# A three-layer graph convolution on one core: four buffers for left-over rows, another order of the work, and the last bias from ScalarE

## What is computed

```python
h = jnp.maximum(_layernorm(x), 0.0)                      # input of conv 1
a = gelu(layer_norm(gcn_conv(h, W1, b1), gamma1, beta1))  # conv 1
c = layer_norm(gcn_conv(a, W2, b2), gamma2, beta2)        # conv 2
x = x + gelu(c + h)
h = jnp.maximum(_layernorm(x), 0.0)
out = x + gcn_conv(h, W3, b3)                             # conv 3
# gcn_conv: segment_sum(dinv[s] * dinv[d] * (x @ W)[s], d) + b, with a self loop for every node
```

## Time and profile before

| | |
|---|---|
| median of the runs | 3902.14 us |
| profiled execution, its own time | 3909.11 us |
| its span (first to last instruction) | 3907.3 us |
| mean granted clock of TensorE | 0.931 |
| busy share of the span: PE, PEld, DVE, ACT, POOL | 79%, 65%, 71%, 46%, 63% |
| instructions | 58757 |
| preamble, about | 0 to 435 us |
| conv 1, about | 435 to 1389 us |
| conv 2, about | 1389 to 2908 us |
| conv 3, about | 2908 to 3907 us |

### The profile page before, as it was taken

How to read it: one execution, slowest core, us unless ns; L and a number is a source line. 1 busy time by engine, 2 the same in 40 slices (tenths; PEclk the granted TensorE clock), 3 DMA queues, 4 the chain that set the end, 5 groups by cost and what they waited for, 6 DMA issues and landing times. The chain is left out here.

```text
span 3907.3 us, 58757 instructions
## 1 busy us (share of the span) xinstructions
PE 3089.9 (79%) x15721; PEld 2521.0 (65%) x15721; DVE 2763.0 (71%) x6384; ACT 1780.0 (46%) x2611; POOL 2449.4 (63%) x1853
## 2 busy tenths in 40 slices
PE   8133599999999957777777777777759999999999
PEld 2122487777777746666666666666647777777777
DVE  9899688778888857666666666666646656566665
ACT  0365466666666635555555555555541122111111
POOL 0122466666666647666666666666648887888877
PEclk9999999999999989888888888888869999999999
DMA  2599777777777747777677677777748888888886
GB/s 108 225 412 416 254 206 197 195 204 198 196 202 196 186 143 217 212 213 202 206 215 209 198 213 213 203 210 210 210 148 246 247 253 255 251 257 252 258 248 202
DMA packets 321118, 867.69 MB, mean 222 GB/s; under 512 B 78801, under 2 KB 79987, under 8 KB 321064
## 3 DMA queue, kind: packets, MB, share of 16 engines
q1 hardware_dynamic: 190120, 682.00, 47.8%
q0 software_dynamic: 130944, 185.08, 26.8%
HBM read 653.10 MB, written 307.81 MB: 246 GB/s over the span
## 5 line engine op out<-in xcount | busy, mean ns | idle before, releaser
L835 POOL DMA_INDIRECT gathered<-H,idx x1062 | 1567.7, 1476 | 430.6 <-issue 253.8
L894 ACT ACTIVATE ahi<-agg 128x1024 fp32r<-128x1024 f32 x354 | 360.7, 1019 | 1136.3 <-PE agg L1184 1099.3
L1204 PE MATMUL out<-Wlo,ahi 128*128 128x512 f32 x2832 | 835.7, 421 | 0.0
L1204 PE MATMUL out<-Whi,ahi 128*128 128x512 f32 x2832 | 834.5, 420 | 0.0
L1204 PE MATMUL out<-Whi,alo 128*128 128x512 f32 x2832 | 792.5, 403 | 26.7 <-DVE alo L1013 26.3
L1184 PE MATMUL agg<-sv,vhi 128*128 128x256 f32 x1416 | 418.1, 323 | 456.2 <-DVE sv L1007 456.0
L1005 DVE TENSOR_TENSOR vlo<-gathered,vhi 128x512 fp32r<-128x512 f32 x354 | 352.3, 995 | 504.5 <-ACT vhi L888 479.4
L1204 PEld LDWEIGHTS out<-Wlo,ahi 128*128 128x128 f32 x2832 | 585.2, 207 | 137.2
L1204 PEld LDWEIGHTS out<-Whi,alo 128*128 128x128 f32 x2832 | 558.5, 199 | 173.2 <-DVE alo L1013 50.6
L1021 DVE BATCH_NORM_STATS2 small<-out 128x6 f32<-128x512 f32 x472 | 317.2, 693 | 435.0 <-PE out L1210 428.9
L1184 PEld LDWEIGHTS agg<-sv,vhi 128*128 128x128 f32 x1416 | 295.3, 209 | 498.3 <-DVE vlo L1005 481.0
(11 more groups left out here) (169 smaller groups left out, 3528.9 us busy)
## 6 DMA issues: line engine op xcount, KB each, us to landing
gathered<-H SPq DMA_DIRECT2D x351, 512.0 KB
H<-ho SPq DMA_DIRECT2D x250, 512.0 KB, 9.5
x<-in_x_dram SPq DMA_DIRECT2D x165, 512.0 KB, 8.7
X<-x SPq DMA_DIRECT2D x117, 512.0 KB
x<-X SPq DMA_DIRECT2D x117, 512.0 KB
out_dram<-conv SPq DMA_DIRECT2D x117, 512.0 KB
H<-x SPq DMA_DIRECT2D x48, 512.0 KB, 9.6
gathered<-H,idx POOLq DMA_INDIRECT x1062
```

What stands on the lines that cost most here:

```text
L835: pool.indirect_dma_start(rows[c], None, H[q][0:N, :], bass.IndirectOffsetOnAxis(ap=own[:, c:c + 1], axis=0), bounds_check=N - 1, oob_is_e ...
L894: nc.scalar.activation(Ahi[p.slot(2)][:, :], Agg[p.slot(2)][:, :], ACT.Copy)\
L1204: m = nc.tensor.matmul(o, a[u][:, c:c + P], w[q][:, f, :], start=(n == 0 and not first), stop=(not second and n == 3 * KD - 1), skip_group ...
```

## The change

- `V` has four buffers in place of two; `gather` is split into `gather_over` (the left-over rows of pair p+4, which wait for `Vlo` of pair p) and, behind it, `gather_first` (the two adding transfers of pair p+3). `v_in` has four semaphores. The row numbers (`indices`) are made five pairs ahead instead of four, and later in DVE's turn.
- The selection matrix is one `tensor_scalar` in place of a `scalar_tensor_tensor` with a tensor of ones.
- Conv 2 on DVE: `over_low(p+2)` is now the first thing of the turn, then `low(p+1)`, `stats(p)`, `indices(p+5)`, and the rest; `normal` is split by halves with `x2_scale` and `x2_shift` between. ACT makes `over_high(p+3)` behind `high(p+2)`. POOL's `residual(p)` waits until DVE has made the selection of pair p+2.
- Conv 3: ACT seeds `Out` with the bias (`seed`), DVE's `result` adds the input rows `Xt` directly, and POOL has no sums left.
- In the preamble the one-hot tiles and `placeb` lie in the new buffers of V, and there are four one-hot tiles instead of three.

```diff
-        gathered = sb("gathered", [P, 10, D])
+        gathered = sb("gathered", [P, 12, D])
-        V = [gathered[:, 8 + u, :] for u in range(2)]
+        V = [gathered[:, 8 + u, :] for u in range(4)]
...
+                    def gather_over(known, p, k):
+                        if has(known, k - 4):
+                            pool.wait_ge(vlo_done.sem, vlo_done.upto(p.after(-4)))
+                        pool.wait_ge(idx_made.sem, idx_made.upto(p))
+                        pool.sem_inc(gather_go, 1)
+                        gather(p, 2, V[p.slot(4)][:, :], v_in, ALU.bypass)
+                    def gather_first(p):
+                        pool.wait_ge(idx_made.sem, idx_made.upto(p))
+                        pool.wait_ge(self_in.of(p), self_in.upto(p))
+                        pool.sem_inc(gather_go, 1)
+                        for j in range(2):
+                            gather(p, j, SelfP[p.slot(4)][:, j, :], g_in, ALU.add)
...
                     def residual(known, p):
+                        if has(known, 2):
+                            pool.wait_ge(sv_made.sem, sv_made.upto(p.after(2)))
...
                         if second and (has(known, 0) or has(known, -2)):
                             power(p)
+                        if has(known, 4):
+                            gather_over(known, p.after(4), 4)
                         if has(known, 3):
-                            gather(known, p.after(3), 3)
-                        if third and has(known, 1):
-                            residual(None if known is None else known + 1, p.after(1))
+                            gather_first(p.after(3))
...
-                            nc.scalar.activation(Out[2 * p.slot(2) + j][:, :], bias_b[0][:, :], ACT.Copy,
+                                taken = res_done if third else cg_done
+                                act.wait_ge(taken.sem, taken.upto(p.after(-2), j + 1))
+                            nc.scalar.activation(Out[2 * p.slot(2) + j][:, :], bias_b[q][:, :], ACT.Copy,
...
-                        nc.vector.scalar_tensor_tensor(Sv[p.slot(2)][:, :], col[:, :], over_to[:, bass.ds(p.n, 1)],
-                                                       ones[:, :], ALU.is_equal, ALU.mult).then_inc(sv_made.sem, 1)
+                        nc.vector.tensor_scalar(Sv[p.slot(2)][:, :], col[:, :], over_to[:, bass.ds(p.n, 1)],
+                                                None, ALU.is_equal).then_inc(sv_made.sem, 1)
...
                     def result(known, p):
+                        dve.wait_ge(xt_in.of(p), xt_in.upto(p))
...
-                            dve.wait_ge(rb_done.sem, rb_done.upto(p, j + 1))
...
-                                                           dinv[:, bass.ds(p.n * 2 + j, 1)], RP[p.slot(2)][:, j, :],
+                                                           dinv[:, bass.ds(p.n * 2 + j, 1)], XtP[p.slot(4)][:, j, :],
...
                     # DVE body
+                            over_low(p)
+                            low(p)
+                            indices(p.after(4))
+                            over_low(p.after(1))
                         if has(known, 2):
                             over_low(p.after(2))
                         if first and has(known, -1):
+                            for j in range(2):
+                                normal(of(known, -1), p.after(-1), j)
+                        if first and has(known, 0):
+                            stats(p)
+                        if has(known, 1):
+                            low(p.after(1))
+                        if second and has(known, 0):
+                            stats(p)
+                        if has(known, 5):
+                            indices(p.after(5))
+                        if second and has(known, -2):
+                            v = x2_var_eps(p.after(-2))
...
                         if third:
                             if has(known, 0):
                                 result(known, p)
                             return
                         if has(known, 0):
                             mean_var(p)
                             var_eps(p)
                             centre(p)
+                        if first:
+                            return
+                        if has(known, -2):
+                            x2_scale(p.after(-2))
+                        if has(known, 0):
+                            normal(known, p, 0)
+                        if has(known, -2):
+                            x2_shift(p.after(-2))
+                        if has(known, 0):
+                            normal(known, p, 1)
+                        if has(known, -1):
+                            x2_sum(of(known, -1), p.after(-1))
+                            x2_mean(p.after(-1))
```

More of the change, by code:

```diff
@@ L831, in gather @@
                         pool.sem_inc(gather_go, 1)
[L832 to L838, removed]
+                        for j in range(2):
+                            gather(p, j, SelfP[p.slot(4)][:, j, :], g_in, ALU.add)
                     def residual(known, p):
-                        R, Xt = RP[p.slot(2)], XtP[p.slot(4)]
-                        if second and has(known, -2):
-                            pool.wait_ge(mean2_done.sem, mean2_done.upto(p.after(-2)))
+                        R = RP[p.slot(2)]
+                        if has(known, 2):
+                            pool.wait_ge(sv_made.sem, sv_made.upto(p.after(2)))
                         for j in range(2):
[L846 to L854, removed]
-                                nc.gpsimd.tensor_tensor(R[:, j, :], Xt[:, j, :], bias_b[2][:, :], ALU.add)\
-                                    .then_inc(rb_done.sem, 1)
+                            pool.wait_ge(r_done.sem, r_done.upto(p, j + 1))
+                            nc.gpsimd.tensor_tensor(R[:, j, :], R[:, j, :], beta_b[1][:, :], ALU.add)\
+                                .then_inc(rb_done.sem, 1)
                     def power(p):
@@ L959, in body @@
                         if known == 0:
-                            if first:
+                            if not second:
                                 seed(0, p)
-                            for k in range(2):
-                                over_high(p.after(k))
-                                if k == 0 or second:
-                                    high(p.after(k))
+                            over_high(p)
+                            high(p)
+                            over_high(p.after(1))
                             if second:
+                                high(p.after(1))
+                                over_high(p.after(2))
                                 relu_x(0, p)
@@ L970, in body @@
                                 squares(p.after(-2))
-                            if has(known, 2):
-                                over_high(p.after(2))
                             if has(known, 1):
@@ L976, in body @@
                                 high(p.after(2))
+                            if has(known, 3):
+                                over_high(p.after(3))
                             if has(known, -2):
@@ L985, in body @@
                             over_high(p.after(2))
-                        if first and has(known, 1):
+                        if has(known, 1):
                             seed(of(known, 1), p.after(1))
@@ L1226, in convolution @@
                 landed.close()
-            if not third:
+            if second:
+                root_in.close()
+                for flag in (r_done, rb_done, x2_done, mean2_done, sq2_done, sc2_done, co2_done):
+                    flag.close()
+            else:
+                seeded.close()
+            if third:
+                res_done.close()
+            else:
                 for flag in (st_done, mv_done, cg_done, y_done, gelu_done, h_done):
```

126 lines of the change are left out of this document (44 added, 82 removed).

## The result

The changed kernel takes 3728.45 us (median of 4 runs, 3724.05 to 3730.7), beside 3898.92 us for the kernel before (now the median of 4 runs, 3895.04 to 3906.1, where the part ahead had three): a ratio of 0.9559, 95% interval 0.9541 to 0.9578. It is faster by 4.4% where I forecast 9.8%, and lies outside my range of 3430 to 3680. The span is 3725.5 us.

What follows compares the result with a forecast made beforehand. Conv 2 was held by a chain through the selection, TensorE nearest its floor in conv 1 and 3. 3909.1 - 68 (conv 1) - 212 (conv 2) - 98 (conv 3) - 5 (starts) = 3526, median 3519, said 3520; range 3430 to 3680.

Steps and rivals of the forecast that it cites:

- the third rival: All convolutions: the tensor_scalar selection is held for a whole transfer instruction each turn, conv 1 loses 14 us, total 3601; chance 0.10.
- (19.7 + 1.0 + 0.8) / 2 = 10.75 us a turn: Conv 2: 19.7 us for two turns, plus 1.0 landing and 0.8 clock, halved; gain 212 us.
- The loop: Conv 2: POOL's gathers of pair p+3 follow power(p) and feed TensorE before power(p+2); 19.7 us for two turns.
- the wait at L1177: Conv 2: TensorE waits for the gathers at the transposes, some 2 us a turn, 150 to 300 us in all.
- landing: Conv 2: time from the last gather's issue until its rows arrive, 3.7 us, with 1.0 added, halfway to 5.7.
- the clock: Conv 2: TensorE's clock falls behind waits of 2 us, adding 0.8 us to each pass of the two-turn loop.
- the other two terms: Conv 2: start of power to end of the third transfer, 6.74 us; last matmul to next power, 1.50 us.
- The lower bound of 9.87 us a turn: Conv 2: shortest turn allowed for the two-turn loop, a gain of 315 us.
- The second: Rival: late gathers take most of the selection's gain, conv 2 at 11.75 us a turn, total 3697; chance 0.18.
- None reaches the present 12.56, so there is a gain: Conv 2: each engine's own turn, TensorE 7.77, DVE 9.0, POOL 9.4, DMA 8.9 us, lies below the present turn.
- the first rival: All convolutions: all waits go and the clock stays full, conv 2 at 9.87 us a turn, total 3384; chance 0.12.
- the fourth: Rival: TensorE gets only 1.2 GHz through conv 2, which loses 349 us, total 4080, slower than before; chance 0.05.

## Why the prediction was right or wrong

**Conv 1 was right**, to 1 us of 68, and by its mechanism: TensorE waits 0.6 us for `sv` and no longer for `alo`, and with two buffers' waits the gain is gone. How the gain divides between the buffers and the first place, no run tells. The new form of `sv` takes (groups by line, conv 1 of the changed kernel) 0.38 us, where I took 0.35:

```profile
L1010 DVE TENSOR_SCALAR sv<-col,over_to 128x256 fp32r<-128x256 f32 x118 | 44.6, 378 | 0.0
```

That also settles the third rival: 116 of these 118 overlap a transfer instruction of POOL (1.0 us or more), their median is 351 ns and the longest takes 524, so none is held for a whole one; and the old form gives the same time. The rule of the Trainium skill, SBUF — State Buffer, "Who interferes with whom", that a `tensor_scalar` in the mode with both ports and an instruction of GpSimd lock each other out for a whole instruction, had no such effect on the selection here; whether the selection ran in that mode, no run shows. Beside POOL's sums DVE is held for most of a sum (the copy of 3.40 us above).

**Conv 3 was right in its mechanism** and 16 us too small: I had added 0.15 us a turn for queues at a DMA share of 0.94. The share is 0.94 and the turn 7.30. That loads made this far ahead hide their queues is my reading; no run tests it.

**Conv 2 was wrong in the size of two terms, and its whole gain hung on them.** The step that failed is "(19.7 + 1.0 + 0.8) / 2 = 10.75 us a turn". The loop was named rightly, with the wait at L1177 that would replace the other; the turn is 12.69. First, landing: I took 3.7 us from the left-over gather, a plain copy, and 5.7 as the upper end. What the loop waits for is the second adding gather, and it lands in 7.5. The larger part is its place: in this order it is issued into SP's four transfers, and away from them the same gather lands in 3.0. Moving two of the four behind it takes 1.4 us off. That it adds costs some 0.5 to 0.7 us of landing there. The trace of the kernel before could have told, in its timeline ahead of the earlier trace rows:

```profile
2304.86 1.76 POOL L835 DMA_INDIRECT gathered<-H,idx  x1 [0.30 <-issue]
...
2307.30 0.36 SPq L794 DMA_DIRECT2D H<-ho  x1
...
2310.84 0.70 SPq L777 DMA_DIRECT2D x<-in_x_dram  x1
```

There the second adding gather is issued by 2306.62, ahead of SP's burst, and the left-over one, from which I took the 3.7 us, ends at 2307.98, only 0.7 us into it. The change makes an adding gather the last: now the burst is at 1921.21 to 1924.83 and this gather ends at 1923.71, 2.5 us into it. I counted the order of the gathers for POOL's time, and not for the place that each gets in DMA.
Second, the clock: 0.8 us a pass, interpolated between waits of 3.0 and 0.68 us. But two turns share one loop, so the wait comes once in two turns, and is 7.3 us long, outside what I interpolated between. The pass behind it takes 9.42 us and not 7.77, 1.65 more. Ten more matmuls give these 1.6 us back; the other 2.2 of the 3.8 us that they take off the double turn are landing, because the gather comes to another place in SP's burst. So the two terms act on each other, and what each experiment takes off does not add up. The Trainium skill, TensorE: Matmul & The Clock Gate, "HAM oscillation", describes just such an iteration, in which every piece starts cold behind a transfer; the trace agrees for the first sums behind the wait (the 8 transposes in 1.97 us, not 1.03).
The sum had to be 19.7 + 5.3: landing 3.8 more, pass 1.65 more, and 0.15 less in the other two terms. (The lower bound of 9.87 us a turn should read 9.85, half of 19.7.)

**The rivals.** The second, the wait that changes its name, was the right one for conv 2, even beyond its upper end of 11.75; its 3697 would have been near, and 3731, for an edit of conv 2 that does nothing, is what came. That this number fits is partly luck: the edit did not do nothing, it took away a wait of 3.0 us in each turn and brought one of 7.3 in every second, and the two loops happen to be almost equally long (12.56 and 12.69 us a turn). I gave the two 0.18. The wrong sentence is "None reaches the present 12.56, so there is a gain": sums of engines bound a turn from below, and say nothing of a loop. Against the first rival stands the wait of 445.2 us, against the fourth the granted clock of 0.83 in conv 2, far from 0.55.

## What to carry to other kernels

When a wait is taken away in a loop where engines feed each other over several turns, write down every closed loop with its length divided by its turns, and take each term from the instruction that stands in it, at the place among other transfers that it will have, not from its neighbour at another place. An added stage of distance (here gathers for p+4, for which the buffers were there already) divides a loop by three instead of two, and brought 309 us, more than all edits of the change together (170). If a wait can only be shortened, look what else is issued at the same time: a few microseconds of order between queues decide how long a transfer takes.

## What I had not expected of the hardware

- The waits of 7.3 us in every second turn cost the clock of the pass behind each: 9.42 us instead of 7.77. Some 1170 added matmuls, of no use but to keep TensorE busy, made the kernel 236 us faster.
- The same adding gather lands 3.0 us after its issue when SP issues nothing near it, and 7.4 us when it ends 2.0 to 2.6 us into four transfers of 512 KB. A copying gather at such a place takes 6.9.
- A gather that adds in place takes POOL 1.7 us of issuing instead of 1.0 to 1.2.
- A copy of 3 numbers a partition on DVE lasted 3.40 us beside POOL's two sums, and POOL's sums 3.10 instead of 2.53. With the copy elsewhere, the next operation of DVE was held as long (means of 1701 ns for the copy before, 1629 for its successor after).
